# Post-norm decoder block in float32: the self-attention stage with x1 written by ScalarE, the row bias as a 129th value column, another order on VectorE, and no loop

## What is computed

```python
qkv = jnp.einsum('bsd,de->bse', x, W_qkv) + b_qkv
q, k, v = jnp.split(qkv, 3, axis=-1)
attn = jnp.einsum('bsd,btd->bst', q, k) * SCALE      # one head, SCALE = 8 ** -0.5
attn = attn * mult(attn)     # 2.0, 1.5, 1.0, 0.3 or 0.1, by the band in which sigmoid(attn) lies
attn = softmax(attn)
out = (attn @ v) @ W_proj + b_proj
x1 = layernorm(x + out)
```

## Time and profile before

| | us |
|---|---|
| median of three runs | 1861.3 (1858.33 to 1861.49) |
| the profiled execution, its own time | 1866.61 |
| span of that execution, first to last instruction | 1864.8 |
| mean granted TensorE clock over the span | 0.92 of full speed |
| last instruction of self attention ends | 186.94 |
| VectorE, TensorE busy over the span | 82%, 90% |
| ScalarE, GpSimd busy over the span | 53%, 61% |

### The profile page before, as it was taken

How to read it: one execution, slowest core, us unless ns; L and a number is a source line. 1 busy time by engine, 2 the same in 40 slices (tenths; PEclk the granted TensorE clock), 3 DMA queues, 4 the chain that set the end, 5 groups by cost and what they waited for, 6 DMA issues and landing times. The chain is left out here.

```text
span 1864.8 us, 39003 instructions
## 1 busy us (share of the span) xinstructions
PE 1673.7 (90%) x12350; PEld 1367.3 (73%) x12350; DVE 1528.9 (82%) x2881; ACT 986.9 (53%) x1962; POOL 1146.7 (61%) x912
## 2 busy tenths in 40 slices
PE   6766798889888888699999999979999999999997
PEld 5655677777777777477777777658888888888886
DVE  5998477787787778688888888769999999999996
ACT  2443466666666666355655665534444444444443
POOL 3333465665666665399999999915555555555555
PEclk8886588888888888799999999989999999999999
DMA  4000100000000000300000000000000000000000
GB/s 133 28 28 6 30 6 5 5 4 4 3 4 4 4 3 2 91 1 0 0 0 0 0 0 0 0 1 4 7 9 6 8 6 8 6 8 6 8 6 11
DMA packets 19977, 21.17 MB, mean 11 GB/s; under 512 B 1925, under 2 KB 14278, under 8 KB 19914
## 3 DMA queue, kind: packets, MB, share of 16 engines
q1 hardware_dynamic: 18314, 15.95, 3.0%
q0 software_dynamic: 1088, 4.19, 0.8%
q10 hardware_dynamic: 512, 0.23, 0.0%
HBM read 16.17 MB, written 4.19 MB: 11 GB/s over the span
## 5 line engine op out<-in xcount | busy, mean ns | idle before, releaser
L1463 POOL TENSOR_TENSOR mix_c<-mix_e,mix_rinv 128x1024 f32<-128x1024 f32 x128 | 306.5, 2394 | 297.0 <-ACT mix_rinv L1386 297.0
L1435 DVE TENSOR_REDUCE mix_sg<-mix_e 128x256 f32<-128x1024 f32 x128 | 255.7, 1997 | 39.2 <-ACT mix_e L1381 38.5
L850 POOL TENSOR_TENSOR cross_pl<-cross_p,cross_ph 128x624 f16<-128x624 f32 x128 | 174.9, 1367 | 168.3 <-ACT cross_p L700 168.3
L1064 POOL TENSOR_TENSOR gather_d<-gather_e,gather_rinv 128x1024 f32<-128x1024 f32 x128 | 245.0, 1914 | 49.2 <-DVE gather_rinv L1039 41.3
L1308 PE MATMUL mix_Y<-mix_c,kept_phi 128*128 128x256 f32 x1024 | 263.3, 380 | 5.7 <-POOL mix_c L1463 5.7
L1007 ACT ACTIVATE gather_e<-gather_L 128x1024 f32<-128x1024 f32 x128 | 131.1, 1024 | 156.4 <-PE gather_L L974 156.4
L690 ACT COPY cross_pTl<-cross_Tl 77x1024 f16<-77x1024 f16 x128 | 128.9, 1007 | 133.6 <-PE cross_Tl L616 133.6
L1308 PEld LDWEIGHTS mix_Y<-mix_c,kept_phi 128*128 128x128 f32 x1024 | 175.2, 190 | 19.9 <-POOL mix_c L1463 4.1
L1029 DVE TENSOR_REDUCE gather_mx<-gather_L 128x32 fp32r<-128x1024 f32 x128 | 156.8, 1225 | 36.7 <-PE gather_L L955 30.9
L1035 DVE TENSOR_REDUCE gather_rsum<-gather_e 128x32 f32<-128x1024 f32 x128 | 156.2, 1221 | 30.7 <-ACT gather_e L1007 30.7
L1373 ACT CAST mix_me<-mix_m 128x256 fp32r<-128x256 f32 x128 | 51.7, 404 | 238.5 <-DVE mix_m L1444 238.5
(11 more groups left out here) (214 smaller groups left out, 4637.7 us busy)
## 6 DMA issues: line engine op xcount, KB each, us to landing
attn_xTg<-in_xT SPq DMA_DIRECT2D x16, 256.0 KB, 2.7
kept_xres<-in_x POOLq DMA_DIRECT2D x4, 1024.0 KB, 11.4
out<-mix_res SPq DMA_DIRECT2D x32, 128.0 KB, 1.8
cross_cg<-in_ctxT SPq DMA_DIRECT2D x32, 58.5 KB, 1.7
setup_wT<-in_w_qkvT SPq DMA_DIRECT2D x1, 192.0 KB
kept_consts<-in_consts SPq DMA_DIRECT2D x1, 66.0 KB
first_xq<-in_xq ACTq DMA_DIRECT2D x1, 64.0 KB, 2.7
setup_wproj<-in_w_proj SPq DMA_DIRECT2D x1, 64.0 KB
```

The costliest lines, as they stand in the source:

```text
L850: pool.tensor_tensor(pl[j % 2][:], p32[j % 2][:], ph[j % 2][:], ALU.subtract).then_inc(pl_ready, 1)
L1064: pool.tensor_tensor(dd[tu.par][ju][:].rearrange("p i (n s) -> p i n s", n=16), e[ju][:], rinv[ju][:].rearrange("p (i n) -> p i n", i=2).u ...
L1435: dve.tensor_reduce(sg[j1 % 2][:], e[j1][:].rearrange("p c t -> p t c"), X, ALU.add)\
L1463: pool.tensor_tensor(cc[j3][:], e[j3][:], rinv[j3 % 2][:].unsqueeze(1).to_broadcast([128, 4, 256]), ALU.mult)\
```

## The change

All of it is in self attention, and in two tiles of the setup.

- x1 is no longer made on VectorE (L381) and copied on GpSimd (L252). VectorE makes a [128, 4] tile `shift` = -mean x rstd, and ScalarE writes y x rstd + shift with four instructions straight into `xres`. TensorE's X transposes `xres`.
- `avec` becomes the 129th column of `w2a`, so V and R are one product of 129 columns, and the tile in PSUM takes two banks. `rb` and `vp` are both read from there. `vp` has three buffers in place of two.
- The orders are new. VectorE: band 0 to 2 of k-1, rb and vp of k, rinv, y and statistics of k-2, then band 3, band 5, f2 and mx of k-1, shift of k-2, nb of k-1. ScalarE: uT of k, x1 of k-3, pT of k-2, x1T of k-4, a of k, pr of k-1. TensorE: U and V of k, T of k-2, S of k, O of k-2, X of k-3.
- The hardware loop is gone: all steps, now 20, stand in the program one after the other.

```diff
@@ GpSimd @@
-                    pool.wait_ge(x1_ready, g.after(1, 1))
-                    pool.tensor_copy(w.xres[:, bass.ds(g.n * 512, 512)], x1[g.par][:]).then_inc(x1_kept, 1)
@@ TensorE: U of k stands ahead of this @@
-                        pe.matmul(psV[:, b * 128:(b + 1) * 128], xb, w.w2[:], start=True, stop=True)
-                        ins = pe.matmul(psR[:, b:b + 1], xb, w.avec[:], start=True, stop=True)
+                        ins = pe.matmul(V[:, b // 2, b % 2, :], xTg[g % 2][:, b * 128:(b + 1) * 128], w.w2a[:],
+                                        start=True, stop=True, skip_group_check=True)
                     ins.then_inc(v_made, 1)
+                for g in groups(k, 2):
+                    pe.wait_ge(p_ready, g + 1)
+                    reach(pe, pT_ready, g)
...
+                        ins = pe.transpose(psT[:, c], pr[g % 2][:, c], w.ident)
...
+                for g in groups(k, 0):
+                    pe.wait_ge(uT_ready, g + 1)
+                    reach(pe, a_ready, g)
...
+                        ins = pe.matmul(psS[:, c], uT[:, c], xTg[g % 2][:, c], start=True, stop=True)
...
+                for g in groups(k, 2):
+                    pe.wait_ge(pT_ready, g + 1)
+                    pe.wait_ge(v_ready, g + 1)
+                    reach(pe, mv_ready, g)
...
+                        ins = pe.matmul(psO[:, c], pT[g % 2][:, c], vp[g % 3][:, b, :], start=True, stop=True)
@@ ScalarE @@
+                for g in groups(k, 3):
+                    act.wait_ge(shift_ready, g + 1)
+                    for b in range(GB):
+                        ins = act.activation(w.xres[:, residual(g)][:, b * 128:(b + 1) * 128], y[g % 2][:, b, :],
+                                             ACT.Identity, bias=shift[g % 2][:, b:b + 1], scale=rstd[g % 2][:, b:b + 1])
+                    ins.then_inc(x1_ready, 1)
@@ VectorE @@
+                for g in groups(k, 1):
+                    dve.wait_ge(a_ready, g + 1)
...
+                for g in groups(k, 0):
+                    dve.wait_ge(v_made, g + 1)
+                    reach(dve, a_ready, g)
+                    dve.tensor_scalar(rb[:].rearrange("p (i b) -> p i b", i=2), V[:, :, :, 128], w.beta[:], SCALE,
+                                      ALU.add, ALU.mult).then_inc(rb_ready, 1)
...
+                for g in groups(k, 2):
...
+                    dve.wait_ge(p_ready, g + 1)
+                    reach(dve, mv_ready, g)
+                    dve.reciprocal(rinv[:], sums[g % 2][:]).then_inc(y_chain, 1)
+                    dve.wait_ge(o_made, g + 1)
...
+                for g in groups(k, 1):
+                    dve.wait_ge(band_done, 3 * g + 1)
+                    dve.scalar_tensor_tensor(out=band[3][:], in0=av, scalar=T_085, in1=band[0][:],
+                                             op0=ALU.is_gt, op1=ALU.add).then_inc(band_done, 1)
...
+                for g in groups(k, 2):
+                    dve.wait_ge(rstd_ready, g + 1)
+                    reach(dve, x1_ready, g - 1)
+                    dve.scalar_tensor_tensor(out=shift[g % 2][:], in0=mv[g % 2][:, :, 0], scalar=-1.0,
+                                             in1=rstd[g % 2][:], op0=ALU.mult, op1=ALU.mult).then_inc(shift_ready, 1)
+                for g in groups(k, 1):
+                    dve.wait_ge(mx_done, g + 1)
+                    dve.tensor_scalar(nb[g % 2][:], mx[:], -0.5, None, ALU.mult).then_inc(f_ready, 1)
-                    for b in range(GB):
-                        ins = dve.tensor_scalar(x1[g.par][:, b * 128:(b + 1) * 128], y[g.par][:, b, :],
-                                                mv[g.par][:, b, 0:1], rstd[g.par][:, b:b + 1],
-                                                ALU.subtract, ALU.mult)
```

More of the change, by code:

```diff
@@ L206, in attention @@
         uT = st.sb("uT", [128, 512])
-        vp = [st.sb(f"vp{i}", [128, 512]) for i in range(2)]
+        vp = [st.sb(f"vp{i}", [128, GB, 128]) for i in range(3)]
         rb = st.sb("rb", [128, GB])
@@ L242, in _ @@
                     .then_inc(x_loaded[q], 16)
[L244 to L247, removed]
+            for k in STEPS:
+                for g in groups(k, 1):
+                    pool.wait_ge(band_done, 3 * g + 1)
                     pool.tensor_tensor(band[4][:], band[1][:], band[2][:], ALU.add).then_inc(low_ready, 1)
-                g = k - 3
-                if g.within(GROUPS):
-                    pool.wait_ge(x1_ready, g.after(1, 1))
-                    pool.tensor_copy(w.xres[:, bass.ds(g.n * 512, 512)], x1[g.par][:]).then_inc(x1_kept, 1)
[L253 to L258, removed]
@@ L259, in _ @@
-            steps(pool, GROUPS, 3, step)
+                for g in groups(k, 2):
+                    pool.wait_ge(mv_ready, g + 1)
+                    pool.tensor_tensor(veps[:], mv[g % 2][:, :, 1], w.eps[:, 0:GB], ALU.add).then_inc(pool_chain, 1)
+                    pool.wait_ge(pool_chain, g + 1)
+                    reach(pool, x1_ready, g - 1)
+                    pool.tensor_tensor(rstd[g % 2][:], veps[:], w.neg_half[:, 0:GB], ALU.pow).then_inc(rstd_ready, 1)
         @block.sync
         def _(sync):
[L263 to L267, removed]
@@ L268, in _ @@
-            steps(sync, GROUPS, 0, step)
+            for g in range(GROUPS):
+                reach(sync, s_made, g - 1)
+                sync.dma_start(xTg[g % 2][:], io["xT"][:, residual(g)]).then_inc(xT_loaded[g % 2], 16)
         @block.tensor
         def _(pe):
[L272 to L279, removed]
+            for k in STEPS:
+                for g in groups(k, 0):
+                    pe.wait_ge(xT_loaded[g % 2], 16 * (g // 2 + 1))
+                    reach(pe, uT_ready, g)
+                    pe.matmul(psU[:], w.m[:], xTg[g % 2][:], start=True, stop=True).then_inc(u_made, 1)
+                    reach(pe, v_ready, g)
+                    reach(pe, rb_ready, g)
@@ L349, in step @@
                     ins.then_inc(p_ready, 1)
-                g = k - 3
-                if g.within(GROUPS):
-                    act.wait_ge(x1T_made, g.after(1, 1))
-                    act.copy(w.x1T[:, bass.ds(g.n * 512, 512)], psX[:]).then_inc(x1T_kept, 1)
-            steps(act, GROUPS, 3, step)
         @block.vector
@@ L362, in _ @@
                               w.mask[:].rearrange("a (b t) -> a b t", t=J), 1.0, FILL, ALU.subtract, ALU.mult)
[L364 to L370 removed]
+            for k in STEPS:
+                for g in groups(k, 1):
+                    dve.wait_ge(a_ready, g + 1)
+                    reach(dve, f_ready, g)
+                    av = a[g % 2][:]
                     dve.tensor_scalar(band[0][:], av, T_095, 2.0, ALU.is_gt, ALU.add)
```

196 lines of the change are left out of this document (75 added, 121 removed).

## The result

The change makes the kernel slower. Its median is 1911.35 us (1903.94 to 1916.2, 4 runs) against 1861.39 us for the kernel before, measured together with it (1858.33 to 1861.78, 4 runs): ratio 1.0269, interval 1.0233 to 1.0304, or +50 us. Forecast was +24.5 us and a time of 1886, with 1904 as the upper end of the range. The direction is right, the size is half of what was measured, and the median lies above the range.

What follows compares the result with a forecast made beforehand. VectorE bound self attention before; afterwards a closed loop would. Start 42.0, 14 periods of 11.2 and a 12.6 tail end the stage at 211.4, not 186.94: +24.5 on 1861.3, called 1886 us; range 1872 to 1904.

Steps and rivals of the forecast that it cites:

- by its busy time alone a step would be 7.4 us: VectorE's self-attention step: 9.84 us less the work removed gives 7.1, with some added waits between dependent operations 7.4 us.
- The closed loop, y to nb: On VectorE, from y of group k-2 to the end of nb of k-1: 5.40, with one more wait 5.45 us.
- The closed loop, nb to y: Same group through exponentials, T, pT and O to y: 6.44 us at the low clock, 5.15 at the full one.
- The period: Self-attention time per group: 11.9 us at the low clock, 10.6 at the full one, 11.2 taken, against 9.84 before.
- the rival with the low clock throughout: Self attention at period 11.9, 10 us more than forecast, time 1896; chance 0.22 together with the port rule's version.
- The start: Start of self attention: y of group 0 at 36.5 (35 to 38), nb of group 1 at 42.0.
- The tail: From nb of group 15 to self attention's end: 12.39 us before, 12.6 with the shift.
- x1 on ScalarE, four in 1.1 us: ScalarE insertion between exponentials and pT: four instructions priced as a, 368 ns each, overlapping to 1.1 us, hidden under S.
- Band 5 to 0.69, no price for rstd on VectorE: VectorE in self attention: band 5 falls from 960 ns to 0.69 us; GpSimd's rstd and veps beside it add nothing.
- the rival that put 18 us on VectorE: Port rule: rstd and veps hold up band 5 and f2, 18 us more, 1904; chance 0.22 together with low clock.
- The third vp buffer and the second bank of V at nothing: In self attention, the added vp buffer and second PSUM bank of V were costed at nothing.
- I cost the unrolling ... at nothing: Self attention's loop ran only twice over four steps, 11 of 19 steps already unrolled; writing out the rest costed nothing.

Runs made afterwards that it cites:

- the last version: Changed kernel with y last, band 3 behind bands 0 to 2, shift behind mx, x1 behind a, 72 waits, X one step later: 1838.78 us, ratio 0.9855.
- y last: Changed kernel with rinv, y and statistics at the end of VectorE's step, shift a step later: 1869.27 us, ratio 1.0048; with 72 waits 1856.22 us, 0.9975.
- before + 184 waits: Kernel before with 184 waits on an already reached semaphore, on TensorE at the head of cross attention: 1883.5 us, ratio 1.0136.
- the unrolled kernel: Kernel before with self attention written out step by step, no other change: 1873.38 us, ratio 1.0056; with 88 already reached waits on TensorE 1865.69 us, ratio 1.0008.
- the 72 waits: Changed kernel with 72 waits on an already reached semaphore, on TensorE at the head of cross attention: 1897.26 us, ratio 1.0175.
- 256 (reached in two ways): Kernel before with 256 already reached waits on TensorE at cross attention's head: 1875.47 us, ratio 1.0063; or changed kernel with 72: 1897.26 us, 1.0175.
- 512: Kernel before with self attention unrolled (424 instructions) and 88 already reached waits on TensorE at the head of cross attention: 1865.69 us, ratio 1.0008.

## Why the prediction was right and wrong, point by point

- **VectorE bound the stage before; by its busy time alone a step would be 7.4 us.** Borne out as far as the last version shows it: with the loop open, VectorE is busy 11.1 us of 12 and a step takes 7.94, of which 7.94 x 11.1 / 12 = 7.3 busy.
- **The closed loop, y to nb.** Forecast 5.45, measured 5.41.
- **The closed loop, nb to y.** Forecast 6.44 at the low clock, measured 6.42; T starts 1.73 us after nb ends in both, O 4.35 for the forecast 4.3. The exponentials, T, pT and O do stand in a row, and moving y to the end of the step (-36 us in the stage) or O ahead of S (-16) shortens it as the loop says. The mechanism is shown.
- **The period.** Forecast 11.2 as the middle of 10.6 and 11.9, measured 11.56, midway between the forecast and the rival with the low clock throughout. A term mis-sized by 0.36 us or 14 x 0.36 = 5 us: after TensorE's pause S takes 1.75 to 2.07 us, near the low clock's 1.91, and T 1.11 in most turns and 0.66 to 0.79 in some; O is between 1.17 and 2.08. The mean granted clock is 0.76 and 0.81, but the links of the loop lie mostly in the low part. The mean over a stretch is not the clock of the links.
- **The start.** Y of group 0 at 33.72, forecast 36.5 (35 to 38), nb of group 1 at 38.95 instead of 42.0 at its end: 2.9 us early. The tail, from the end of nb of group 15 to the stage's end, took 13.87 us for the forecast 12.6, 1.3 more; there x1 on ScalarE has nothing to hide under, and its start to the start of X takes 2.26 us, where x1 on VectorE took 1.18. So -2.9 + 5 + 1.3 makes the 3.4 by which the stage came out too long, +27.95 for +24.5: that it came this near is in part luck, as the errors offset each other.
- **x1 on ScalarE, four in 1.1 us.** Wrong: 1.64. Scale and bias are both tiles with a value per partition here, and the source is y in SBUF, where a has its source in PSUM; which of these costs the 0.5 us was not tried. It fell under S, as forecast: pT's end at 124.19 lies just before O can start behind S, so the price was 0 to 0.1 us in a period, and some 1 us once, in the tail.
- **Band 5 to 0.69, no price for rstd on VectorE.** Right: band 5 and f2 take 692 ns each with rstd beside them. But the evidence was read too widely. What falls on GpSimd is seen in groups by line, 60 to 180 us:

```profile
L261 POOL TENSOR_TENSOR attn_rstd<-attn_veps,kept_neg_half 128x4 f32<-128x4 f32 x11 | 16.1, 1464 | 0.9
L407 DVE TENSOR_TENSOR attn_f<-attn_band,attn_a 128x512 f32<-128x512 f32 x11 | 7.6, 692 | 0.4
L404 DVE TENSOR_TENSOR attn_band<-attn_band 128x512 f32<-128x512 f32 x11 | 7.6, 692 | 0.4
L258 POOL TENSOR_TENSOR attn_veps<-attn_mv,kept_eps 128x4 f32<-128x4 f32 x10 | 5.6, 556 | 61.4 <-DVE attn_mv L396 61.4
```

  Rstd took 1.07 us beside passes with one input and takes 1.46 beside passes with two; veps goes from 0.29 (at 98.90 in the kernel before) to 0.56. It is GpSimd that is held, and nothing waits for it but the last shift, as the last x1 did before (1.40 us in both), so the rival that put 18 us on VectorE had the wrong engine. With y last, shift meets the other case, and VectorE is the one that waits for band 4 on GpSimd to end (1.14 us for four elements, 0.15 elsewhere):

```profile
92.64 1.25 POOL L255 TENSOR_TENSOR attn_band<-attn_band 128x512 f32<-128x512 f32 x1
92.78 1.14 DVE L377 SCALAR_TENSOR_TENSOR attn_shift<-attn_mv,attn_rstd 128x4 f32<-128x4 f32 x1
```

  The Trainium skill ("SBUF — State Buffer", section "SBUF: two separate sides") has it that of two such operations the one that starts first holds the port and the other blocks. Two rows of this case agree. Shift starts behind GpSimd's band 4 and ends with it, and veps (117.06) starts behind VectorE's band 3 and ends at 117.62, with that pass (117.56): the later one loses, on either engine. Rstd agrees only in part: it starts behind band 5 (117.59) and is held, but f2 starts at 118.32, inside rstd, and still takes 0.69.
- **The third vp buffer and the second bank of V at nothing.** In the change's profile nothing waits for either, as forecast. But in the new order two buffers would put vp between O and y, 0.97 us in the loop, so the buffer belongs to the order. The bank of V was not tried by itself.
- **"I cost the unrolling ... at nothing"; "the later stages stand behind the block's end and shift as they are."** This is the step that failed. Written-out steps change the place of all later code, and with it whether the loop of cross attention is fetched anew in its turns. Bringing the place on costs (before + 184 waits: 21 us, 4 of them the waits), taking it away gives back 14 to 17 us in the change, 13 with y last, and 8 in the unrolled kernel. The unrolling itself costs nothing that was measured (ratio 1.0008). The term put at nothing was thus worth 15 to 19 us in the change, against the 5 us of the period.

The sum: with the place mended the change is still 32.7 us above the kernel before that was measured with it (1864.52): 28 in the stage, 1.3 for the 72 waits, 3.4 left. From 50 to 32.7 is 17.3, and with the waits' 1.3 the place is worth 18.6. So 28 for the closed loop, 18.6 for the place and 3.4 that I can't place make up the 50. The size of the middle term is the least certain. The two profiles of this pair differ by 11.5 us, and in the stretch of cross attention by 12.0, of which 5.8 are idle time of TensorE; the other 6.2 are its busy time, which runs from 492 to 511 us over all profiles, with the granted clock and not with the packets. Executions of one kernel differ by 3 to 25 us here, four runs of the change are few for that, and only the shortest of them was profiled; whether the others fetched in more turns is not on record.

Two things stay open. Which places of the loop are bad: 184 and 424 instructions further on are, 256 (reached in two ways) and 512 are not, and in between nothing was tried. And why only some turns fetch, two in the change's profile and three in the other four with the loop in a bad place. For the first the Trainium skill offers a rule ("Runtime: NRT & Kernel Launch", section "Instruction fetch mechanics"): instructions are held in blocks of 16 KiB, 256 instructions, and a taken branch to a target outside the current window of two blocks has to wait for a DMA. The packets of 16 KB agree, and so do the placements, as 256 and 512 are whole blocks by it. The window of two does not: a turn that is fetched anew takes nine packets here, yet in the kernel before the loop turns for over 340 us without one, so more than two blocks must be held. How many, no run here shows. My counts of instructions are from the program as built, and a few the assembler may add are not in them.

## What to carry to other kernels

When an operation moves ahead in an engine's step, ask in which step its input's last producer now stands: if the operation and what follows it lead back to that producer through the other engines, the loop's length is the least period, however much busy time was saved, and its links are to be priced at the clock at which they begin. Moving the operation to the end of the step took 36 of the stage's 215 us. When code ahead of a hardware loop grows or shrinks, look at the instruction packets and at TensorE's idle time in the later loops before and after, not at the stage's length, which the clock blurs; a few instructions that do nothing may give the place back.

## What was unexpected of the hardware

- A loop that fits in one placement was fetched anew in some turns in another: 18 or 19 packets of 16 KB against 37 to 46, with waits of up to 3.2 us in the change, and 4.0 in the unrolled kernel, that end with no semaphore. A turn that is fetched anew takes nine packets. More instructions made the kernel faster: 72 more, 14 us less.
- A wait for a semaphore that is long reached is not free for TensorE: 72 add 1.3 us at the head of the block, 184 add 4.0, 256 add 8.1; loads cover part of it.
- The granted clock can change from one step to the next: the kernel with O ahead of S takes T at 1.11 and 0.66 us in neighbouring steps, and its steps take 11.04 and 9.68 us.
- Four activations of 128x128 from SBUF with a tile for the scale and one for the bias take 1.64 us, the four of a from PSUM, with a tile for the bias alone, 1.14 (at 124.58 in the change).
